# Scan phase: the feed-forward weight quantised in its turned layout, its scales brought back as rows through memory

## The chip, the cores and the metric

The kernel runs on one core of one Trainium2 chip. The metric is the device time of one execution in microseconds; the median of the runs shown is used. The profile is of one execution, recorded by the hardware profiler.

## The reference, cut to what matters

Two layers work on x, 2 x 4096 tokens of 512 channels. The first adds to x a gated state-space branch and a quantised linear map; the second is a linear attention with a gated feed-forward part. The change touches only how the weight of the quantised map is prepared:

```
xn = layernorm(x)
x  = x + _L0_attn_ref(xn, ...) + _L0_ffn_ref(xn, weight, bias)

# in _L0_ffn_ref: weight is [512 out, 512 in]
blocks = weight.reshape(512, 16, 32)                  # blocks of 32 along the input channel
scales = maximum(max(abs(blocks), axis=-1) / 7.5, 1e-30)
wd     = nearest_on_fp6_grid(blocks / scales) * scales
out    = xd @ wd.T + bias                             # xd: the input, quantised in the same way
```

The product contracts over the input channel, so TensorE wants the weight with the input channel on the partitions ("turned"), while a block of 32 lies along the input channel.

## The kernel before, in words

Four phases run one after the other on each engine: project (the first two weight products), scan (the state-space recurrence), mix (the sums of layer one and the first half of layer two) and the second layer. The change is in the scan phase, phase_scan (L648 to L915).

The scan loops over 64 octets o of 8 channels each. TensorE makes three f32 products per octet, each 128x128 by 128x512: `own` of the next octet (L885, into bank SB), the Toeplitz product (L903) and the product with the states (L906, both into bank YB). In program order they are own(o+1), L903 of o, L906 of o. VectorE scans the bank of own(o+1) into c_state (L757, two instructions); L906 of octet o+1 waits for them. ScalarE takes the finished bank out (`take`, L827) and issues the store of it to scr_y (L831) on its own DMA queue. GpSimd writes the three masked tables of an octet (L739), three octets ahead at most; own(o) waits for the tables of o. SyncE loads z (L701) six octets ahead.

Everything else of the scan phase is hung onto octets by constants, at the end of an octet's step on the engine in question. VectorE's step of octet o is: the scan of o+1 first, then what hangs on o. So a wait in what hangs on o holds up the scan of o+2. ScalarE's step of octet o is take(o), then DMA issues and copies that hang on o, then the store of o.

The feed-forward weight in this scheme:
- ScalarE loads it in its natural layout, output channel on the partitions, in four DMAs of 256 KB (L844) at o = 1 to 4, into c_wf_nat, [128, 2048].
- VectorE quantises it in nine steps at o = 10 to 18 (L771 to L794): the maximum over blocks of 32 (L776), scale (L778), reciprocal (L780), the product with the inverse scale (L782), exponent bits (L784), rounding constant (L787), addition (L789), subtraction (L791), product with the scale (L793). L784 and L787 have one tensor as input, L782, L789, L791 and L793 two.
- TensorE turns it at o = 24 to 27 (`turn_weight`, L888): four transposes of 128x128 an octet into one of the banks 0 to 3.
- ScalarE copies each bank as the high part of the split weight one octet later (L860), VectorE subtracts it for the low part another octet later (L808).
- The weights w2 and wk are split in the same way from SBUF at o = 32 to 39 (L836 and L762). Their pieces, and those of wv, are loaded by ScalarE at every second octet from o = 6 to 28 (L854).
- GpSimd clears two accumulators and a column at its octet 20 (L743).

Of the kernel before, what the change touches and what calls it, by code (L numbers as in the profile page):

```python
# [3 lines left out]
P = 128  # L4
# [643 lines left out]
def phase_scan(nc, sh, ins, scr, keep, banks, areas, late, mix):  # L648
# [5 lines left out]
    def sem(name):  # L654
        return nc.alloc_semaphore(name)
# [9 lines left out]
    q_scale = first_weight.tile("c_q_scale", [P, KT * D // QBLOCK])  # L665
    q_inv = first_weight.tile("c_q_inv", [P, KT * D // QBLOCK])
# [3 lines left out]
    w2_raw, wk_raw = late["w2_raw"], late["wk_raw"]  # L670

    z_in = [sem(f"c_z_in{i}") for i in range(Z)]
    y_stored = [sem(f"c_y_stored{i}") for i in range(Y)]
# [5 lines left out]
    wf_in = sem("c_wf_in")  # L679
    w_hi, w_lo = keep["w_hi"], keep["w_lo"]  # L680
    HI = 2 * KT
    q_step, f_turned, f_hi = sem("c_q_step"), sem("c_f_turned"), sem("c_f_hi")

    FB, YB, SB = banks[0:4], banks[4:6], banks[6:8]
    into_t, toep_t, out_pow, mask8 = keep["into_t"], keep["toep_t"], keep["out_pow"], keep["mask8"]
    ident = keep["ident"]
    z_of = scr["z"].rearrange("(o c) r n -> o (c r) n", c=OCTET)
    y_of = scr["y"].rearrange("(o c) m n -> o (c m) n", c=OCTET)
    TURN_AT, WEIGHTS_AT, QUANTISE_AT = 24, 32, 10
    QUANTISED_AT, WEIGHT_PIECES_AT, BIASES_AT = 1, 6, 30  # L690
    MIX_IN_AT, MIX_PREPARE_AT, MIX_BANKS_AT, MIX_HEAD_AT = 38, 40, 42, 61
    MIX_TURN_AT = {56: 0, 60: 1}
# [57 lines left out]
    def vector(dve):  # L750
        def scan(o):
            dve.wait_ge(own_full, o + 1)
            if o >= 2:
                dve.wait_ge(y_full, o - 1)
            rate = keep["decay"][:, o:o + 1].broadcast_to([P, NCB - 1])
            for b in range(B):
                nc.vector.tensor_tensor_scan(state[o % 2][:, b, 1:], rate, SB[o % 2][:, b * NCB:(b + 1) * NCB - 1],  # L757
                                             0.0, ALU.mult, ALU.add).then_inc(state_done, 1)

        def weight_low(i, kt, tile, raw):  # L760
            dve.wait_ge(w_hi, HI + KT * i + kt + 1)
# [3 lines left out]
        blocks = wf_nat[:, :].rearrange("p (b e) -> p b e", e=QBLOCK)  # L765
        NB = KT * D // QBLOCK

        def wide(tile):
            return tile[:, :].unsqueeze(2).broadcast_to([P, NB, QBLOCK])

        def quantise_step(k):  # L771
            dve.wait_ge(wf_in, 16 * KT)
            if k:
                dve.wait_ge(q_step, k)
            if k == 0:
                ins_ = nc.vector.tensor_reduce(q_max[:, :], blocks, AX.X, ALU.max, apply_absolute_value=True)  # L776
            elif k == 1:
                ins_ = nc.vector.tensor_scalar(q_scale[:, :], q_max[:, :], 1.0 / FP6_MAX, SCALE_EPS, ALU.mult, ALU.max)  # L778
            elif k == 2:
                ins_ = nc.vector.reciprocal(q_inv[:, :], q_scale[:, :])  # L780
            elif k == 3:
                ins_ = nc.vector.tensor_tensor(blocks, blocks, wide(q_inv), ALU.mult)  # L782
            elif k == 4:
                ins_ = nc.vector.tensor_scalar(q_work[:, :].bitcast(U32), wf_nat[:, :].bitcast(U32), EXPONENT_BITS,  # L784
                                               None, ALU.bitwise_and)
            elif k == 5:
                ins_ = nc.vector.tensor_scalar(q_work[:, :], q_work[:, :], 1.0, ROUND_MAGIC, ALU.max, ALU.mult)  # L787
            elif k == 6:
                ins_ = nc.vector.tensor_tensor(wf_nat[:, :], wf_nat[:, :], q_work[:, :], ALU.add)  # L789
            elif k == 7:  # L790
                ins_ = nc.vector.tensor_tensor(wf_nat[:, :], wf_nat[:, :], q_work[:, :], ALU.subtract)  # L791
            else:
                ins_ = nc.vector.tensor_tensor(blocks, blocks, wide(q_scale), ALU.mult)  # L793
            ins_.then_inc(q_step, 1)  # L794

        for i in range(2):
            nc.vector.memset(state[i][:, :, 0:1], 0.0).then_inc(zeroed, 1)
        dve.wait_ge(zeroed, 2)
        scan(0)
        for o in range(NO):  # L800
            if o + 1 < NO:
                scan(o + 1)
            if QUANTISE_AT <= o < QUANTISE_AT + 9:
                quantise_step(o - QUANTISE_AT)
            if TURN_AT <= o - 2 < TURN_AT + KT:
                kt = o - 2 - TURN_AT
                dve.wait_ge(f_hi, kt + 1)
                nc.vector.tensor_tensor(wf[:, 1, kt, :], FB[kt][:, :], wf[:, 0, kt, :].bitcast(F32), ALU.subtract)\  # L808
# [12 lines left out]

    def scalar(act):
# [17 lines left out]
        for o in range(NO):  # L840
            take(o)
            if QUANTISED_AT <= o < QUANTISED_AT + KT:
                t = o - QUANTISED_AT
                act.dma_start(wf_nat[:, t * D:(t + 1) * D], ins["L0_ffn_weight"][t * P:(t + 1) * P, :])\  # L844
                   .then_inc(wf_in, 16)
            if o == WEIGHT_PIECES_AT:
                for h in range(2):
                    act.wait_ge(*project["z"][h])
                    act.wait_ge(*project["v"][h])
                act.wait_ge(*project["powers"])  # L850
            if WEIGHT_PIECES_AT <= o < WEIGHT_PIECES_AT + 2 * 3 * KT and (o - WEIGHT_PIECES_AT) % 2 == 0:
                i, kt = divmod((o - WEIGHT_PIECES_AT) // 2, KT)
                tile, name, done = pieces[i]
                act.dma_start(tile[:, kt, :], ins[name][:, kt, :]).then_inc(done, 16)  # L854
            if o in (BIASES_AT, BIASES_AT + 2, BIASES_AT + 4):
                mix["load_bias"]((o - BIASES_AT) // 2)
            if TURN_AT <= o - 1 < TURN_AT + KT:
                kt = o - 1 - TURN_AT
                act.wait_ge(f_turned, kt + 1)
                nc.scalar.activation(wf[:, 0, kt, :], FB[kt][:, :], ACT.Copy).then_inc(f_hi, 1)  # L860
            if WEIGHTS_AT <= o < WEIGHTS_AT + 2 * KT:
                i, kt = divmod(o - WEIGHTS_AT, KT)
                weight_high(i, kt, *((w2, w2_raw), (wk, wk_raw))[i])
# [1274 lines left out]
def two_layer_kernel(nc, ins, out):  # L2138
# [3 lines left out]
    def dram(name, shape, dt=F32):  # L2142
# [118 lines left out]
```

## Time and profile before

| | us |
|---|---|
| median of 3 runs (2083.98 to 2085.03) | 2084.08 |
| the profiled execution, its own time | 2084.98 |
| its span, first to last instruction | 2083.2 |
| TensorE busy in it | 2065.6 |
| VectorE busy in it | 1521.2 |
| ScalarE busy in it | 1095.3 |
| GpSimd busy in it | 839.5 |

Span and busy times are of the profiled execution; 1.8 us of its time lie around the span, and it is 0.9 us longer than the median. A matmul in f32 is recorded as two instructions, so its rows say x2, and a row's duration is to the end of the last one, beyond the start of the next.

### The profile page before, as it was taken

The numbers are of one execution on the slowest core, as the hardware profiler recorded it, in microseconds if no ns is written. First come the engines' busy times: TensorE is split into PE (matmuls) and PEld (weight loads), VectorE is DVE, ScalarE is ACT, GpSimd is POOL, SyncE is SP. The second block draws the span as 40 slices with busy tenths as digits, with TensorE's granted clock in tenths as the row PEclk, the third lists the DMA queues.
The fourth block names the chain that finished last, engine by engine and source line by source line (L and its number), as shares of the span: only waits on it lengthen the run. The fifth ranks groups of instructions, "written<-read, shape, count | busy, mean of one in ns | idle before, by whom it ended". The sixth has DMA issues, their size and how long they took to land.

```text
span 2083.2 us, 27336 instructions
## 1 busy us (share of the span) xinstructions
PE 2065.6 (99%) x9263; PEld 1647.1 (79%) x9263; DVE 1521.2 (73%) x2943; ACT 1095.3 (53%) x1842; POOL 839.5 (40%) x842
## 2 busy tenths in 40 slices
PE   9999999999999999999999999999999999999998
PEld 7787888444688888888888888788888888888887
DVE  5898785666687777777777875677777676667776
ACT  4555556323455555555555555754455555555453
POOL 1001110355545444454445453144444444444444
PEclk9999999999999999999999999999999999999999
DMA  5997883886533333333333333422222222222211
GB/s 186 235 222 221 202 219 116 280 255 211 178 115 118 102 118 105 116 118 102 122 107 117 103 128 104 152 71 72 71 71 71 92 91 81 92 71 72 71 41 41
DMA packets 193637, 263.46 MB, mean 126 GB/s; under 512 B 34265, under 2 KB 124633, under 8 KB 190938
## 3 DMA queue, kind: packets, MB, share of 16 engines
q1 hardware_dynamic: 180376, 238.18, 37.7%
q10 hardware_dynamic: 13122, 23.53, 3.0%
q8 instruction: 74, 1.21, 0.2%
q14 instruction: 65, 0.53, 0.1%
HBM read 160.88 MB, written 100.79 MB: 126 GB/s over the span
## 4 chain that ended last, share of the span: by engine, by line
PE 89%; DVE 5%; ACT 2%; issue 2%; POOL 1%; DMA 1%; SPq 0%; POOLq 0%; ACTq 0%
PE bank L102 23%; PE bank L104 23%; PE bank L103 22%; PE bank L1496 7%; PE bank L2052 3%; PE bank L885 3%; PE bank L906 3%; PE bank L903 3%; PE bank L1452 2%; PE bank L629 1%; DVE e_w_lo L1879 0%; DVE d_x L1348 0%; DVE d_xq L1319 0%; DVE d_stats L1350 0%; PE bank L1510 0%
## 5 line engine op out<-in xcount | busy, mean ns | idle before, releaser
L102 PE MATMUL bank<-e_ring,e_w_hi 128*128 128x512 f32 x512 | 200.8, 392 | 0.0
L103 PE MATMUL bank<-e_ring,e_w_hi 128*128 128x512 f32 x512 | 199.3, 389 | 0.0
L104 PE MATMUL bank<-e_ring,e_w_lo 128*128 128x512 f32 x512 | 199.3, 389 | 0.0
L1496 PE MATMUL bank<-d_kh,d_nat 128*128 128x512 f32 x768 | 191.1, 398 | 0.0
L1772 POOL TENSOR_TENSOR e_x<-e_x,e_beta 128x512 f32<-128x512 f32 x64 | 91.3, 1446 | 220.7 <-ACT e_y L1815 220.7
L1117 POOL TENSOR_TENSOR rstd<-d_var_eps,neg_half 128x1 f32<-128x1 f32 x64 | 35.6, 556 | 340.5 <-DVE d_var_eps L1359 340.5
L1826 ACT ACTIVATE e_kr<-bank 128x512 f32<-128x512 f32 x64 | 38.0, 593 | 247.6 <-PE bank L104 247.6
L1496 PEld LDWEIGHTS bank<-d_kh,d_nat 128*128 128x128 f32 x768 | 139.7, 188 | 26.9
L1897 DVE TENSOR_TENSOR e_ring<-e_mixed,e_ring 128x512 fp32r<-128x512 f32 x128 | 93.5, 731 | 88.1 <-ACT e_ring L1790 88.0
L1754 POOL TENSOR_TENSOR e_x<-e_x,e_ff 128x512 f32<-128x512 f32 x64 | 83.3, 1302 | 175.6 <-DVE e_ff L1963 175.6
L1364 DVE TENSOR_TENSOR d_nat<-d_xn,d_nat 128x512 fp32r<-128x512 f32 x64 | 85.9, 1344 | 77.7 <-ACT d_nat L1224 77.7
L1888 DVE SCALAR_TENSOR_TENSOR e_mixed<-e_xt,cols,e_prev 128x512 f32<-128x512 f32 x128 | 104.0, 813 | 41.3 <-ACT e_prev L1801 40.7
L1206 ACT ACTIVATE d_xt<-bank 128x512 f32<-128x512 f32 x64 | 38.2, 597 | 166.9 <-PE bank L1452 166.9
L757 DVE TENSOR_TENSOR_SCAN c_state<-decay,bank 128x255 f32<-128x255 f32 x128 | 80.5, 670 | 52.8 <-PE bank L885 52.6
L308 POOL TENSOR_TENSOR b_rstd<-b_var_eps,neg_half 128x4 f32<-128x4 f32 x16 | 16.2, 1010 | 255.0 <-DVE b_var_eps L364 255.0
L102 PEld LDWEIGHTS bank<-e_ring,e_w_hi 128*128 128x128 f32 x512 | 96.1, 188 | 20.4 <-issue 0.9
L1790 ACT ACTIVATE e_ring<-e_mixed 128x512 fp32r<-128x512 f32 x128 | 80.7, 632 | 59.8 <-DVE e_mixed L1888 57.5
L1758 POOL TENSOR_TENSOR e_y<-e_y,e_att 128x512 f32<-128x512 f32 x64 | 107.0, 1671 | 12.8 <-DVE e_att L1982 12.8
L104 PEld LDWEIGHTS bank<-e_ring,e_w_lo 128*128 128x128 f32 x512 | 96.1, 188 | 20.0
L103 PEld LDWEIGHTS bank<-e_ring,e_w_hi 128*128 128x128 f32 x512 | 96.1, 188 | 19.3
L102 PE MATMUL bank<-e_w_hi,e_keys 128*128 128x512 f32 x256 | 103.7, 405 | 0.1
L102 PE MATMUL bank<-b_xt,b_v 128*128 128x512 f32 x256 | 100.8, 394 | 2.7 <-ACT b_vt L557 2.7
(222 smaller groups left out, 6298.0 us busy)
## 6 DMA issues: line engine op xcount, KB each, us to landing
scr_v<-b_vt SPq DMA_DIRECT2D x64, 256.0 KB, 3.5
scr_z<-b_zt SPq DMA_DIRECT2D x64, 256.0 KB, 5.6
c_z<-scr_z SPq DMA_DIRECT2D x64, 256.0 KB, 4.3
scr_y<-c_y ACTq DMA_DIRECT2D x64, 256.0 KB, 3.9
d_x<-in_L_attn_x SPq DMA_DIRECT2D x64, 256.0 KB, 3.8
d_v<-scr_v SPq DMA_DIRECT2D x32, 512.0 KB, 5.1
scr_x<-d_x SPq DMA_DIRECT2D x64, 256.0 KB, 2.3
scr_xnt<-d_xt SPq DMA_DIRECT2D x32, 512.0 KB, 4.1
```

The lines of the kernel that those rows point to most:

```text
L102: eng.matmul(out, lhs[hi], rhs[hi], start=first, stop=False, skip_group_check=onto)
L103: eng.matmul(out, lhs[hi], rhs[lo], start=False, stop=False, skip_group_check=onto)
L104: return eng.matmul(out, lhs[lo], rhs[hi], start=False, stop=last, skip_group_check=onto)
L757: nc.vector.tensor_tensor_scan(state[o % 2][:, b, 1:], rate, SB[o % 2][:, b * NCB:(b + 1) * NCB - 1], 0.0, ALU.mult, ALU.add).then_inc(sta ...
L1364: nc.vector.tensor_tensor(nat[q][:, 1, :], xn[N % 2][:, :], nat[q][:, 0, :].bitcast(F32), ALU.subtract).then_inc(nat_lo, 1)
L1496: mm = pe.matmul(BG[c][:, :], s[:, i, cols], r[:, j, :], start=M % NTB == 0 and i == j, stop=M % NTB == NTB - 1 and i == 1, skip_group_che ...
L1754: nc.gpsimd.tensor_tensor(x2[h][:, t, :], x2[h][:, t, :], ff[t % 2][:, :], ALU.add).then_inc(base_done, 1)
L1758: nc.gpsimd.tensor_tensor(y[t][:, :], y[t][:, :], att[t % 2][:, :], ALU.add).then_inc(sum_done, 1)
L1772: nc.gpsimd.tensor_tensor(x2[h][:, t, :], x2[h][:, t, :], beta[:, :], ALU.add).then_inc(shifted, 1)
L1790: nc.scalar.activation(ring[slot][:, 0, kt, :], src, ACT.Copy).then_inc(hi_done, 1)
L1888: nc.vector.scalar_tensor_tensor(mixed[kt % 2][:, :], current(g % 2, kt), mu[:, kt:kt + 1], prev[kt % 2][:, :], ALU.mult, ALU.add).then_in ...
L1897: nc.vector.tensor_tensor(ring[slot][:, 1, kt, :], src, ring[slot][:, 0, kt, :].bitcast(F32), ALU.subtract).then_inc(lo_done, 1)
```

## The change

The host lays the weight out a second time, turned (input channel on the partitions), as the input ffn_turned. The natural copy is still loaded, but serves for the maxima alone.

- VectorE finds the maxima at o = 14 (the same instruction), the scales in four small instructions at o = 15, the inverse scales at o = 16, and at o = 17 turns both in 32x32 blocks with four `transpose` instructions into c_q_turned.
- ScalarE loads the turned weight in four DMAs of 256 KB at o = 7, 9, 11, 13. At o = 18 it stores the turned scales in four DMAs of 16 KB to a new scratch tensor, scr_f_scales [32, 512]. At o = 20 it waits for these stores and issues two loads of 1 MB each: rows of the inverse scales into c_q_work and rows of the scales into c_wf_nat, each of 4 rows of 8 KB, repeated for 32 partitions.
- VectorE quantises the turned weight in six steps at o = 22 to 27, of the same kinds as the last six before; the first waits for both row loads.
- ScalarE and VectorE split it at o = 29 to 33, from SBUF. The sixteen transposes on TensorE are gone, and banks 0 to 3 are not used in the scan by them.

```diff
-    TURN_AT, WEIGHTS_AT, QUANTISE_AT = 24, 32, 10
+    ROUNDED_AT, WEIGHTS_AT, SCALES_AT, SCALES_OUT_AT, ROWS_IN_AT, QUANTISE_AT = 28, 32, 14, 18, 20, 22
+    SCALE_STEPS, QUANTISE_STEPS = 3 + KT, 6
+        def scale_step(k):
+            if k:
+                dve.wait_ge(q_step, min(k, 3))
+            scales = q_cols[:, :, KT * KT:2 * KT * KT]
+            if k == 0:
+                dve.wait_ge(wf_in, 32 * KT)
+                ins_ = nc.vector.tensor_reduce(q_max[:, :], wf_nat[:, :].rearrange("p (b e) -> p b e", e=QBLOCK), AX.X,
+                                               ALU.max, apply_absolute_value=True)
...
+            elif k == 2:
+                ins_ = nc.vector.reciprocal(q_cols[:, :, 0:KT * KT], scales)
+            else:
+                ins_ = nc.vector.transpose(q_turned[:, k - 3, :], q_cols[:, k - 3, :])
+            ins_.then_inc(q_step, 1)
         def quantise_step(k):
+            dve.wait_ge(q_step, SCALE_STEPS + k)
+            wf_turned = wf_raw[:, :, :].rearrange("p k d -> p (k d)")
             if k == 0:
+                dve.wait_ge(wf_in, 16 * (2 * KT + KT + 2))
+                ins_ = nc.vector.tensor_tensor(wf_turned, wf_turned, q_work[:, :], ALU.mult)
             elif k == 1:
+                ins_ = nc.vector.tensor_scalar(q_work[:, :].bitcast(U32), wf_turned.bitcast(U32), EXPONENT_BITS,
+                                               None, ALU.bitwise_and)
...
             else:
+                ins_ = nc.vector.tensor_tensor(wf_turned, wf_turned, wf_nat[:, :], ALU.mult)
...
+            if o == SCALES_OUT_AT:
+                act.wait_ge(q_step, SCALE_STEPS)
+                for s in range(P // QBLOCK):
+                    act.dma_start(scr["f_scales"].rearrange("c (t s i) -> s c t i", t=KT, s=P // QBLOCK)[s],
+                                  q_turned[s * QBLOCK:(s + 1) * QBLOCK, :, :]).then_inc(wf_in, 16)
+            if o == ROWS_IN_AT:
+                act.wait_ge(wf_in, 16 * (2 * KT + KT))
+                for w, tile in enumerate((q_work, wf_nat)):
+                    rows = bass.AP(scr["f_scales"].tensor, w * KT * KT * D,
+                                   [[KT * D, P // QBLOCK], [0, QBLOCK], [1, KT * D]])
+                    act.dma_start(tile[:, :], rows).then_inc(wf_in, 16)
...
+            if WEIGHT_PIECES_AT <= o < WEIGHT_PIECES_AT + 2 * KT and (o - WEIGHT_PIECES_AT) % 2:
+                kt = (o - WEIGHT_PIECES_AT) // 2
+                act.dma_start(wf_raw[:, kt, :], ins["ffn_turned"][:, kt, :]).then_inc(wf_in, 16)
...
-                act.wait_ge(f_turned, kt + 1)
-                nc.scalar.activation(wf[:, 0, kt, :], FB[kt][:, :], ACT.Copy).then_inc(f_hi, 1)
+                act.wait_ge(q_step, SCALE_STEPS + QUANTISE_STEPS)
+                nc.scalar.activation(wf[:, 0, kt, :], wf_raw[:, kt, :], ACT.Copy).then_inc(f_hi, 1)
...
-        def turn_weight(kt):
-            if kt == 0:
-                pe.wait_ge(q_step, 9)
-            for ot in range(KT):
-                mm = pe.transpose(FB[kt][:, ot * P:(ot + 1) * P], wf_nat[:, ot * D + kt * P:ot * D + (kt + 1) * P],
-                                  ident[:, :])
-            mm.then_inc(f_turned, 1)
...
-            if TURN_AT <= o < TURN_AT + KT:
-                turn_weight(o - TURN_AT)
...
+        "f_scales": dram("scr_f_scales", [QBLOCK, D]),
...
+    laid["ffn_turned"] = raw["L0_ffn_weight"].T.reshape(KT, P, 512).transpose(1, 0, 2)
```

## Rows read from the trace of the kernel before

**Rows 1.** The page: busy time by engine, and the chain that ended last.

```profile
PE 2065.6 (99%) x9263; PEld 1647.1 (79%) x9263; DVE 1521.2 (73%) x2943; ACT 1095.3 (53%) x1842; POOL 839.5 (40%) x842
...
PE 89%; DVE 5%; ACT 2%; issue 2%; POOL 1%; DMA 1%; SPq 0%; POOLq 0%; ACTq 0%
```

**Rows 2.** Timeline, TensorE: start, duration, line, count [idle before, releaser].

```profile
376.14 1.02 PE L906 MATMUL bank<-c_state,c_outof 128*128 128x512 f32 x2
...
407.04 1.02 PE L906 MATMUL bank<-c_state,c_outof 128*128 128x512 f32 x2
...
412.19 1.02 PE L906 MATMUL bank<-c_state,c_outof 128*128 128x512 f32 x2
413.48 1.10 PE L885 MATMUL bank<-c_z,c_into 128*128 128x512 f32 x2 [0.27 <-issue]
...
430.34 1.02 PE L906 MATMUL bank<-c_state,c_outof 128*128 128x512 f32 x2
...
441.50 0.60 PE L892 MATMUL bank<-consts,c_wf_nat 128*128 128x128 f32 x4
441.93 1.02 PE L885 MATMUL bank<-c_z,c_into 128*128 128x512 f32 x2
```

**Rows 3.** Timeline, VectorE, while the weight is quantised.

```profile
407.56 0.53 DVE L780 RECIPROCAL c_q_inv<-c_q_scale 128x64 f32<-128x64 f32 x1
408.95 1.26 DVE L757 TENSOR_TENSOR_SCAN c_state<-decay,bank 128x255 f32<-128x255 f32 x2 [0.87 <-PE bank L885]
410.13 2.26 DVE L782 TENSOR_TENSOR c_wf_nat<-c_wf_nat,c_q_inv 128x2048 f32<-128x2048 f32 x1
412.31 1.25 DVE L757 TENSOR_TENSOR_SCAN c_state<-decay,bank 128x255 f32<-128x255 f32 x2
413.49 1.33 DVE L784 TENSOR_SCALAR c_q_work<-c_wf_nat 128x2048 uint32<-128x2048 uint32 x1
...
415.91 1.20 DVE L787 TENSOR_SCALAR c_q_work<-c_q_work 128x2048 f32<-128x2048 f32 x1
...
418.36 2.27 DVE L789 TENSOR_TENSOR c_wf_nat<-c_wf_nat,c_q_work 128x2048 f32<-128x2048 f32 x1
...
421.72 2.40 DVE L791 TENSOR_TENSOR c_wf_nat<-c_wf_nat,c_q_work 128x2048 f32<-128x2048 f32 x1
...
425.21 2.26 DVE L793 TENSOR_TENSOR c_wf_nat<-c_wf_nat,c_q_scale 128x2048 f32<-128x2048 f32 x1
```

**Rows 4.** Timeline, GpSimd, two of the table products.

```profile
400.42 0.40 POOL L739 TENSOR_TENSOR c_into<-into_t,consts 128x128 f32<-128x128 f32 x1 [1.46 <-PE bank L906]
...
410.72 1.94 POOL L739 TENSOR_TENSOR c_into<-into_t,consts 128x128 f32<-128x128 f32 x1 [1.46 <-PE bank L906]
```

**Rows 5.** The lines that make the low parts of the split weights, VectorE.

```profile
L808 DVE TENSOR_TENSOR d_wf<-bank,d_wf x4: 662/664/667, 447.2 to 455.8; 128x512 fp32r<-128x512 f32 x4
...
L762 DVE TENSOR_TENSOR d_w<-d_w_raw,d_w x4: 691/691/693, 465.2 to 472.9; 128x512 fp32r<-128x512 f32 x4
```

**Rows 6.** Timeline, ScalarE: a take and the DMA issue that hangs on it.

```profile
408.10 0.60 ACT L827 ACTIVATE c_y<-bank 128x512 f32<-128x512 f32 x1 [1.98 <-PE bank L906]
408.10 0.35 ACTq L854 DMA_DIRECT2D d_w_raw<-in_L_attn_w_w  x1
```

**Rows 7.** DMA issues: count, KB each, median us to landing.

```profile
c_z<-scr_z SPq DMA_DIRECT2D x64, 256.0 KB, 4.3
...
e_w_raw<-in_L_attn_Wq SPq DMA_DIRECT2D x1, 1024.0 KB, 5.0
...
scr_rows<-mean SPq DMA_DIRECT2D x14, 2.0 KB, 11.6
```

**Rows 8.** Stretches: busy us (instructions), TensorE's granted clock, DMA share, GB/s.

```profile
62.00:66.00 4.00, 4.00 (x12) 3.17 (x11) 3.93 (x6) 1.74 (x3) 0.00 (x0) 0.57 0.97 210
66.00:70.00 4.00, 4.00 (x20) 3.26 (x19) 3.93 (x4) 2.08 (x4) 0.00 (x0) 1.00 1.03 388
```

**Rows 9.** Timeline, TensorE, the idle time ahead of the first of these.

```profile
61.42 0.50 PE L102 MATMUL bank<-b_xt,b_v 128*128 128x512 f32 x1 [2.72 <-ACT b_vt L557]
```

More of the change, by code:

```diff
@@ L664, in phase_scan @@
     q_max = first_weight.tile("c_q_max", [P, KT * D // QBLOCK])
-    q_scale = first_weight.tile("c_q_scale", [P, KT * D // QBLOCK])
-    q_inv = first_weight.tile("c_q_inv", [P, KT * D // QBLOCK])
+    q_cols = first_weight.tile("c_q_cols", [P, KT, QBLOCK])
+    q_turned = first_weight.tile("c_q_turned", [P, KT, QBLOCK])
     wf_nat = turned_x.tile("c_wf_nat", [P, KT * D])
@@ L669, in phase_scan @@
     w2, wf, wk, wv = late["w2"], late["wf"], late["wk"], late["wv"]
-    w2_raw, wk_raw = late["w2_raw"], late["wk_raw"]
+    w2_raw, wf_raw, wk_raw = late["w2_raw"], late["wf_raw"], late["wk_raw"]
     z_in = [sem(f"c_z_in{i}") for i in range(Z)]
@@ L681, in phase_scan @@
     HI = 2 * KT
-    q_step, f_turned, f_hi = sem("c_q_step"), sem("c_f_turned"), sem("c_f_hi")
-    FB, YB, SB = banks[0:4], banks[4:6], banks[6:8]
+    q_step, f_hi = sem("c_q_step"), sem("c_f_hi")
+    YB, SB = banks[4:6], banks[6:8]
     into_t, toep_t, out_pow, mask8 = keep["into_t"], keep["toep_t"], keep["out_pow"], keep["mask8"]
-    ident = keep["ident"]
     z_of = scr["z"].rearrange("(o c) r n -> o (c r) n", c=OCTET)
     y_of = scr["y"].rearrange("(o c) m n -> o (c m) n", c=OCTET)
-    TURN_AT, WEIGHTS_AT, QUANTISE_AT = 24, 32, 10
+    ROUNDED_AT, WEIGHTS_AT, SCALES_AT, SCALES_OUT_AT, ROWS_IN_AT, QUANTISE_AT = 28, 32, 14, 18, 20, 22
+    SCALE_STEPS, QUANTISE_STEPS = 3 + KT, 6
     QUANTISED_AT, WEIGHT_PIECES_AT, BIASES_AT = 1, 6, 30
@@ L763, in weight_low @@
                                     ALU.subtract).then_inc(w_lo, 1)
[L765 to L769, printed above, removed]
+        def scale_step(k):
[6 more added lines that the diff above has]
+                                               ALU.max, apply_absolute_value=True)
+            elif k == 1:
+                for t in range(KT):
+                    ins_ = nc.vector.tensor_scalar(scales[:, t, :].rearrange("p (s k) -> p k s", k=KT),
+                                                   q_max[:, t * KT * KT:(t + 1) * KT * KT]
+                                                   .rearrange("p (k s) -> p k s", k=KT),
+                                                   1.0 / FP6_MAX, SCALE_EPS, ALU.mult, ALU.max)
+            elif k == 2:
[3 more added lines that the diff above has]
+            ins_.then_inc(q_step, 1)
@@ L771, in quantise_step @@
         def quantise_step(k):
-            dve.wait_ge(wf_in, 16 * KT)
-            if k:
-                dve.wait_ge(q_step, k)
+            dve.wait_ge(q_step, SCALE_STEPS + k)
+            wf_turned = wf_raw[:, :, :].rearrange("p k d -> p (k d)")
             if k == 0:
-                ins_ = nc.vector.tensor_reduce(q_max[:, :], blocks, AX.X, ALU.max, apply_absolute_value=True)
+                dve.wait_ge(wf_in, 16 * (2 * KT + KT + 2))
+                ins_ = nc.vector.tensor_tensor(wf_turned, wf_turned, q_work[:, :], ALU.mult)
@@ L777, in quantise_step @@
             elif k == 1:
-                ins_ = nc.vector.tensor_scalar(q_scale[:, :], q_max[:, :], 1.0 / FP6_MAX, SCALE_EPS, ALU.mult, ALU.max)
+                ins_ = nc.vector.tensor_scalar(q_work[:, :].bitcast(U32), wf_turned.bitcast(U32), EXPONENT_BITS,
+                                               None, ALU.bitwise_and)
             elif k == 2:
-                ins_ = nc.vector.reciprocal(q_inv[:, :], q_scale[:, :])
+                ins_ = nc.vector.tensor_scalar(q_work[:, :], q_work[:, :], 1.0, ROUND_MAGIC, ALU.max, ALU.mult)
@@ L781, in quantise_step @@
             elif k == 3:
-                ins_ = nc.vector.tensor_tensor(blocks, blocks, wide(q_inv), ALU.mult)
+                ins_ = nc.vector.tensor_tensor(wf_turned, wf_turned, q_work[:, :], ALU.add)
             elif k == 4:
[L784 to L791, printed above, removed]
+                ins_ = nc.vector.tensor_tensor(wf_turned, wf_turned, q_work[:, :], ALU.subtract)
@@ L792, in quantise_step @@
             else:
-                ins_ = nc.vector.tensor_tensor(blocks, blocks, wide(q_scale), ALU.mult)
+                ins_ = nc.vector.tensor_tensor(wf_turned, wf_turned, wf_nat[:, :], ALU.mult)
             ins_.then_inc(q_step, 1)
@@ L802, in vector @@
                 scan(o + 1)
-            if QUANTISE_AT <= o < QUANTISE_AT + 9:
+            if SCALES_AT <= o < SCALES_AT + 3:
+                scale_step(o - SCALES_AT)
+            if o == SCALES_AT + 3:
+                for k in range(3, SCALE_STEPS):
+                    scale_step(k)
+            if QUANTISE_AT <= o < QUANTISE_AT + QUANTISE_STEPS:
                 quantise_step(o - QUANTISE_AT)
-            if TURN_AT <= o - 2 < TURN_AT + KT:
-                kt = o - 2 - TURN_AT
+            if ROUNDED_AT <= o - 2 < ROUNDED_AT + KT:
+                kt = o - 2 - ROUNDED_AT
                 dve.wait_ge(f_hi, kt + 1)
-                nc.vector.tensor_tensor(wf[:, 1, kt, :], FB[kt][:, :], wf[:, 0, kt, :].bitcast(F32), ALU.subtract)\
+                nc.vector.tensor_tensor(wf[:, 1, kt, :], wf_raw[:, kt, :], wf[:, 0, kt, :].bitcast(F32), ALU.subtract)\
                   .then_inc(w_lo, 1)
@@ L854, in scalar @@
                 act.dma_start(tile[:, kt, :], ins[name][:, kt, :]).then_inc(done, 16)
+            if WEIGHT_PIECES_AT <= o < WEIGHT_PIECES_AT + 2 * KT and (o - WEIGHT_PIECES_AT) % 2:
+                kt = (o - WEIGHT_PIECES_AT) // 2
+                act.dma_start(wf_raw[:, kt, :], ins["ffn_turned"][:, kt, :]).then_inc(wf_in, 16)
             if o in (BIASES_AT, BIASES_AT + 2, BIASES_AT + 4):
                 mix["load_bias"]((o - BIASES_AT) // 2)
-            if TURN_AT <= o - 1 < TURN_AT + KT:
-                kt = o - 1 - TURN_AT
-                act.wait_ge(f_turned, kt + 1)
-                nc.scalar.activation(wf[:, 0, kt, :], FB[kt][:, :], ACT.Copy).then_inc(f_hi, 1)
+            if ROUNDED_AT <= o - 1 < ROUNDED_AT + KT:
+                kt = o - 1 - ROUNDED_AT
+                act.wait_ge(q_step, SCALE_STEPS + QUANTISE_STEPS)
+                nc.scalar.activation(wf[:, 0, kt, :], wf_raw[:, kt, :], ACT.Copy).then_inc(f_hi, 1)
             if WEIGHTS_AT <= o < WEIGHTS_AT + 2 * KT:
```

## The prediction

> **What bounds the kernel now.** I read the busy times and the chain first: TensorE is busy for 99% of the span and carries 89% of the chain [rows 1]. So work taken off TensorE counts in full, and time in which TensorE is kept waiting counts in full too. Next the timeline of TensorE in the scan. Its L906 of octet 0 starts at 376.14 and that of octet 12 at 407.04 [rows 2]: 30.90 / 12 = 2.575 us an octet with no gap, three products of 0.858 us. TensorE sets the pace, and L906 of octet o starts at 376.14 + 2.575 o as long as nothing is late. Call this the undisturbed clock.
>
> Two things disturb it before. From L906 of octet 14 (412.19) to that of octet 20 (430.34) 18.15 us pass [rows 2], where six octets take 15.45: **2.70 us are lost** while the long quantising steps run. The rows beside it say why. A table product of GpSimd takes 0.40 us, but the one that starts at 410.72 takes 1.94 and ends when VectorE's L782 ends [rows 3, 4]; the next own starts 1.29 us after L906 instead of 0.86 [rows 2]. L885 is said to wait for "issue", but the tables are what came last. Secondly the transposes: four of them stand 0.43 us in TensorE's row, 441.50 to 441.93 [rows 2], and there are four such groups, **1.72 us**. Together 4.4 us that the change could win at most.
>
> **Part by part.**
>
> The transposes go: -1.72 us, at once, since nothing but TensorE's own work sets those four octets.
>
> The maxima, scales and inverse scales move by four octets. VectorE has 2.575 - 1.18 = 1.39 us an octet beside the scan, whose pitch is 408.95 to 410.13 [rows 3]. A reciprocal of 64 columns takes 0.53 us [rows 3]. The three small scalings more and the four block transposes of 32 columns each are not in the trace; from below nothing, from above 0.53 us each, which would be 2.1 us for the transposes at o = 17. VectorE may run about 1.9 us late before L906 is kept waiting (below), so even that end costs nothing in front of an octet with no step behind it. I take 0.
>
> ScalarE gets ten more DMA issues at 0.35 us [rows 6] and waits twice. Its octet holds 0.60 + 0.35 to 0.70 us of 2.575 [rows 6], so issues are covered. The wait at o = 18 is for VectorE's transposes, which come right after scan(18); it is over before take(18). The wait at o = 20 is for four stores of 128-byte pieces, issued 5 us earlier. Nearest rows: 4.3 us for 256 KB, and 11.6 us for 2 KB in 4-byte pieces [rows 7]. I take the first, as pieces of 128 bytes are 32 times larger than the slow ones; the other end is rival C. Behind that wait stand take(21) and the row loads.
>
> The high and low parts are read from SBUF: VectorE's 0.664 becomes 0.691 us [rows 5], under the same 1.39 us. 0.
>
> The row loads and the first quantising step are the new wait. ScalarE issues the loads with take(20). A take starts 1.06 us after L906 (408.10 against 407.04 [rows 2, 6]), so the issue is at 376.14 + 51.50 + 1.06 = 428.7. VectorE asks for them after scan(23), which starts 1.91 us after L906 of octet 21 (408.95 against 407.04 for octet 12 [rows 2, 3]): 376.14 + 54.08 + 1.91 + 1.18 = 433.3. So **they have 4.6 us to land** before VectorE stops. Then VectorE needs 2.19 us for the product (410.13 to 412.31 [rows 3]) and 1.18 for scan(24); L906 of octet 24 is due at 376.14 + 61.80 = 437.9. TensorE is therefore kept waiting if the loads land after 437.9 - 3.4 = 434.5, or 5.8 us after issue.
>
> They are 2.1 MB. One load of 1 MB lands 5.0 us after its issue [rows 7]. The DMA engines at full share move 388 / 1.03 = 376 GB/s, 23.5 GB/s each of 16 [rows 8]; 1.05 MB is 2.8 us of that, leaving 2.2 us that don't depend on size. Two ends then:
> - spread over 16 engines: 2.2 + 2.10 MB / 376 GB/s = 7.8 us, and with three z loads in between (0.7 us each by the same rate) 9.9;
> - spread over 4 engines: 2.2 + 2.10 / 94 = 24.5 us, with four z loads 27.3.
>
> Every large load of the trace has 128 entries in the outermost dimension at both ends, and reaches the rate of 16 engines. The row loads' source has **4 entries outermost**, each repeated 32 times. If a transfer is dealt out by its outermost dimension, only four shares exist, and engines 5 to 16 get none. No row here shows a transfer with four; I take this end, 25 us, because the only thing in which these loads differ from the row of 5.0 us is just that dimension.
>
> The Trainium skill states this rule in "DMA: Bandwidth & Descriptors", section "Rules for kernel authors": an outermost dimension of size c below 16 confines the whole DMA to at most c engines. By it the loads land some 25 us after issue; by the row of 5.0 us alone, 8 to 10.
>
> Working it out for 25 us: landing 428.7 + 25.0 = 453.7; product and scan 2.19 + 1.18, and 0.1 to L906: 457.2, against 437.9 due: **19.3 us lost**. From there VectorE is the bound for five octets: steps of 1.33, 1.20, 2.27, 2.40, 2.26 us, each 0.08 less in pitch, plus 5 scans of 1.18 = 15.0 us [rows 3], against 5 x 2.575 = 12.9: **2.1 us**. GpSimd's lengthened tables fall into the same octets; TensorE already waits there for VectorE, so I add nothing for them, where before they made the 2.70.
>
> **The clock.** TensorE idles some 19 us in this wait. After an idle 2.72 us [rows 9] the granted clock was 0.57 in the next stretch of 4 us and 1.00 after it [rows 8], that is 0.43 x 4 = 1.7 us of work lost, at the lower level of 1.2 GHz. The two octets right behind the wait have short steps on VectorE, so little of it is covered: **1.6 us**.
>
> Sum: 19.3 + 2.1 + 1.6 - 2.70 - 1.72 = **+18.6 us**. The profiled execution took 2084.98, so 2103.6 for one like it; the median of before is 0.9 lower, which gives 2102.7.
>
> **Rivals.**
>
> A. The loads run on 16 engines. Place: the same wait of VectorE at o = 22. They land after 7.8 to 9.9 us, and L906 of octet 24 is late by 2.0 to 4.1, then 2.1 as above, and at the upper end 1.6 for the clock: 4.1 to 7.8 lost, less 4.4: -0.3 to +3.4, or 2083.8 to 2087.5. That is not slower by more than the 0.2% (4.2 us) that a measurement of this kernel can tell from no change. It decides if the loads land within about 11 us of issue. For it: all MB-sized loads here take 5 us or so [rows 7]. Against it: the four outer entries.
>
> B. The loads even land within 5.8 us, and only the transposes show: the six steps then lose about what they lost before, 2.6 us, and the gain is 1.7: 2082.4. Against it: 2.1 MB at 376 GB/s alone is 5.6 us.
>
> C. The stores of the scales land like the 4-byte ones, 11.6 us after issue [rows 7]. The last is issued at about 425.4, so the wait of ScalarE ends at 437.0, 8.3 us after 428.7; takes and row loads shift by that: 2111 with four engines, 2094 to 2096 with sixteen.
>
> D. The change doesn't keep TensorE free: only if a transpose stayed. The diff leaves none; no chance given.
>
> **Chances.** Forecast 0.79, A 0.12, B 0.02, C 0.07. The forecast's own range comes from 22 us to landing and no loss by the clock (-3.0 - 1.6: 2098) to 27.3 us and a low clock for twice as long (+2.3 + 1.6: 2106.6). I widen it by 3 us below, for a rate per engine that is higher when only four are at work, and up to C: 2095 to 2111. A and B lie outside. Slower by over 0.2%: the forecast, C and a tail of A, 0.87. Within 0.2%: 0.11. Faster: 0.02, since the whole of what could be won, 4.4 us, is just over the bound.
>
> **What would show it.** In the changed profile: no L892 rows; one idle time of TensorE of 15 to 21 us ahead of L906 of octet 24, released by c_state, and VectorE's product waiting for the DMA into c_wf_nat or c_q_work; these loads with 22 to 27 us to landing; a DMA share of about a quarter in that stretch; a granted clock near 0.5 for some us behind it. The loss at octets 14 to 20 should be gone. I am wrong on the main step if the row loads land within 11 us, and on the others if TensorE also stops at octet 20 or 21 (the stores), or if the six steps lose well over 2 us behind the wait.

## The result, and the profile after

The changed kernel takes 2112.55 us (median of 4 runs, 2108.96 to 2114.83) against 2084.03 for the one before in the same comparison: ratio 1.0139, 95% interval 1.0127 to 1.0151, so 1.4% slower. The profiled execution took 2110.73 (span 2108.9), which is 25.75 more than the profiled one of before.

The page of the kernel after, busy times and chain [rows 1]:

```profile
PE 2066.7 (98%) x9247; PEld 1647.0 (78%) x9247; DVE 1520.9 (72%) x2950; ACT 1095.4 (52%) x1842; POOL 837.0 (40%) x842
...
PE 88%; DVE 5%; DMA 2%; ACT 2%; issue 2%; POOL 1%; SPq 0%; POOLq 0%; ACTq 0%; DVEq 0%
```

TensorE's work has not grown; 2% of the chain is now a transfer. Where it stands shows in TensorE's timeline. The numbering has moved: L927 is the product with the states (before: L906), L914 own, L924 the Toeplitz product [rows 2].

```profile
373.90 1.02 PE L927 MATMUL bank<-c_state,c_outof 128*128 128x512 f32 x2
...
412.53 1.02 PE L927 MATMUL bank<-c_state,c_outof 128*128 128x512 f32 x2
...
417.56 1.12 PE L927 MATMUL bank<-c_state,c_outof 128*128 128x512 f32 x2 [2.29 <-DVE c_state L757]
...
440.16 1.12 PE L924 MATMUL bank<-c_z,c_toep 128*128 128x512 f32 x2 [0.90 <-ACT c_y L842]
465.09 2.08 PE L927 MATMUL bank<-c_state,c_outof 128*128 128x512 f32 x2 [23.81 <-DVE c_state L757]
```

I call **slip** the start of that product in octet o, less its start in octet 0 and less 2.575 o: zero on the undisturbed clock. After: 0 up to octet 15 (412.53), 2.46 at 16, 4.26 at 18 to 23 (the second part, 1.80, comes under a low clock; see the stretches below), 29.39 at 24 (465.09), 33.14 at 29, 33.81 at 63. Before, it ends at 5.12. So the scan lost 28.69 us; the phase before it happened to end 2.24 us earlier (octet 0 at 373.90 against 376.14), the phases behind it took 0.70 less, and 28.69 - 2.24 - 0.70 = 25.75.

VectorE, after, with the two stops and the six steps [rows 3]:

```profile
414.05 2.29 DVE L772 TENSOR_REDUCE c_q_max<-c_wf_nat 128x64 f32<-128x2048 f32 x1 [3.49 <-DMA d_wf_raw<-in_ffn_turned]
...
417.42 0.39 DVE L776 TENSOR_SCALAR c_q_cols<-c_q_max 128x16 f32<-128x16 f32 x4
...
421.42 0.47 DVE L783 STREAM_TRANSPOSE c_q_turned<-c_q_cols 128x32 f32<-128x32 f32 x4
...
461.58 2.29 DVE L792 TENSOR_TENSOR d_wf_raw<-d_wf_raw,c_q_work 128x2048 f32<-128x2048 f32 x1 [26.17 <-DMA c_wf_nat<-scr_f_scales]
463.79 1.25 DVE L757 TENSOR_TENSOR_SCAN c_state<-decay,bank 128x255 f32<-128x255 f32 x2
464.96 1.20 DVE L794 TENSOR_SCALAR c_q_work<-d_wf_raw 128x2048 uint32<-128x2048 uint32 x1
```

The maxima wait 3.49 us for a load of the *turned* weight, which they don't read. The product waits 26.17 us for the rows. ScalarE, after, from the stores of the scales on [rows 6]:

```profile
425.57 2.64 ACTq L864 DMA_DIRECT2D scr_f_scales<-c_q_turned  x4
...
430.72 0.60 ACT L842 ACTIVATE c_y<-bank 128x512 f32<-128x512 f32 x1 [0.68 <-PE bank L927]
430.72 0.60 ACTq L871 DMA_DIRECT2D c_q_work<-scr_f_scales  x1
431.36 0.56 ACTq L871 DMA_DIRECT2D c_wf_nat<-scr_f_scales  x1
...
434.19 5.21 ACTq L846 DMA_DIRECT2D scr_y<-c_y  x1
...
439.52 4.21 ACTq L880 DMA_DIRECT2D d_wv<-in_L_attn_Wv  x1
443.78 3.87 ACTq L846 DMA_DIRECT2D scr_y<-c_y  x1
```

The row loads are issued at 430.72 and the product begins at 461.58, 30.9 us later. In the trace the packets of 8 KB are the rows: 256 of them on ScalarE's queue, the first starts at 433.09, the last ends at 460.96. Stretches, after: the last columns are TensorE's granted clock, the DMA share and GB/s [rows 8].

```profile
418.70:422.15 3.45, 3.45 (x5) 1.36 (x5) 2.35 (x8) 0.60 (x1) 1.12 (x3) 0.51 0.66 188
...
430.00:435.00 5.00, 5.00 (x13) 2.28 (x12) 2.37 (x5) 1.23 (x3) 2.25 (x6) 1.00 0.94 267
...
450.00:455.00 5.00, 0.00 (x0) 0.00 (x0) 0.00 (x0) 0.00 (x0) 0.00 (x0) 0.50 0.37 141
455.00:460.00 5.00, 0.00 (x0) 0.00 (x0) 0.00 (x0) 0.00 (x0) 0.00 (x0) 0.50 0.24 103
460.00:465.00 5.00, 0.00 (x0) 0.00 (x0) 3.42 (x4) 0.00 (x0) 0.00 (x0) 0.50 0.21 80
```

Ahead of the landing the DMA share is 0.24, about 4 engines of 16, at 103 GB/s: the four shares of the prediction, seen.

### The profile page after: what moved, and what is told of

It is laid out like the page before. It is cut to its first block, busy times and chain, and to the rows that moved or that the text cites. A ratio compares the mean times of both kernels' runs of the same rounds, so it can differ in the third digit from the quotient of the medians.

```text
span 2108.9 us, 27314 instructions
## 1 busy us (share of the span) xinstructions
PE 2066.7 (98%) x9247; PEld 1647.0 (78%) x9247; DVE 1520.9 (72%) x2950; ACT 1095.4 (52%) x1842; POOL 837.0 (40%) x842
## 4 chain that ended last, share of the span: by engine, by line
PE 88%; DVE 5%; DMA 2%; ACT 2%; issue 2%; POOL 1%; SPq 0%; POOLq 0%; ACTq 0%; DVEq 0%
PE bank L102 23%; PE bank L104 22%; PE bank L103 22%; PE bank L1515 7%; PE bank L2071 3%; PE bank L927 2%; PE bank L914 2%; PE bank L924 2%; PE bank L1471 2%; DMA c_wf_nat<-scr_f_scales 1%; PE bank L629 1%; DVE e_w_lo L1898 0%; DVE d_x L1367 0%; DVE d_xq L1338 0%; DVE d_stats L1369 0%
## 5 line engine op out<-in xcount | busy, mean ns | idle before, releaser
L842 ACT ACTIVATE c_y<-bank 128x512 f32<-128x512 f32 x64 | 38.2, 596 | 145.8 <-PE bank L927 129.6
L103 PEld LDWEIGHTS bank<-e_ring,e_w_hi 128*128 128x128 f32 x512 | 96.2, 188 | 19.3
```

The lines of the kernel that those rows point to most:

```text
L103: eng.matmul(out, lhs[hi], rhs[lo], start=False, stop=False, skip_group_check=onto)
```

## The experiments

In each, the slip is read as above, from the one profiled execution. Those marked "one time" have a single time and no interval; the others are medians of 4 to 11 executions. A ratio is to the kernel before, timed in the same comparison, with its 95% interval.

**rows_16**: each load of 4 x 32 rows becomes four loads of 32 partitions, whose outermost dimension has 32 entries.

```diff
-                    rows = bass.AP(..., w * KT * KT * D, [[KT * D, P // QBLOCK], [0, QBLOCK], [1, KT * D]])
-                    act.dma_start(tile[:, :], rows).then_inc(wf_in, 16)
+                    for s in range(P // QBLOCK):
+                        rows = bass.AP(..., (w * KT + s) * KT * D, [[0, QBLOCK], [1, KT * D]])
+                        act.dma_start(tile[s * QBLOCK:(s + 1) * QBLOCK, :], rows).then_inc(wf_in, 16)
```

> Each row load of 1 MB is cut into four of 32 partitions, so that the outermost dimension is 32 and not 4; bytes, rows and repeats are the same. Theory (a load is dealt out by its outermost dimension, four entries use four DMA engines): all eight land 8 to 10 us after the first issue instead of 31, TensorE's wait ahead of L906's counterpart of octet 24 falls from 24 to 2 to 4 us, and the kernel takes 2088 to 2093 us (the stop at octet 16 stays). Rival (reading one row 32 times, or sharing with the z loads and y stores, makes the loads slow): they land 25 to 31 us after issue as before and the time stays at 2105 to 2115.

Measured: 2096.57, ratio 1.006 (1.0043 to 1.0076), 16.0 us below the change; slip 4.18 at octet 17, 15.54 at 24, 19.94 at 63. The time lies above my range of 2088 to 2093 and below the rival's 2105. The outermost dimension is the main cause, but a stop of 11.4 us stays where I had worked out 2.0 to 4.1 for sixteen engines.

**rows_2** (one time): the opposite, two loads of 64 partitions for each tile, outermost dimension 2 (`[[KT * D, 2], [0, QBLOCK], [1, KT * D]]`).

> The opposite dose: each row load is cut into two of 64 partitions, whose source has 2 entries outermost. Theory: all run on the same two engines, the data need twice as long, the last load lands 50 to 60 us after issue and the kernel takes 2130 to 2145 us. Rival (bytes or repeats set it): landing and time as in the changed kernel, 2109 to 2115.

Measured: 2130.23; slip 53.40 at octet 63. The stretch of rows_2 behind the start of the stop:

```profile
440.00:445.00 5.00, 0.00 (x0) 0.00 (x0) 0.00 (x0) 0.00 (x0) 0.00 (x0) 0.64 0.13 42
```

A share of 0.13 is 2 engines of 16. Its slip comes in two parts, as TensorE's timeline of rows_2 shows:

```profile
458.03 2.07 PE L925 MATMUL bank<-c_z,c_toep 128*128 128x512 f32 x2 [22.04 <-ACT c_y L842]
...
484.35 2.08 PE L928 MATMUL bank<-c_state,c_outof 128*128 128x512 f32 x2 [20.72 <-DVE c_state L757]
```

The first wait is not for the rows but for ScalarE's take of y, whose queue is held up; the next runs show by what.

**own_sem**: the turned loads count on a semaphore of their own, so that neither the maxima nor the row loads wait for them.

```diff
-                dve.wait_ge(wf_in, 32 * KT)
+                dve.wait_ge(wf_in, 16 * KT)
...
-                act.dma_start(wf_raw[:, kt, :], ins["ffn_turned"][:, kt, :]).then_inc(wf_in, 16)
+                act.dma_start(wf_raw[:, kt, :], ins["ffn_turned"][:, kt, :]).then_inc(turned_in, 16)
```

> The turned weight's loads count on a semaphore of their own, so that the maxima at octet 14 wait for the natural weight alone; the row loads stay as they are. Theory: the stop of 2.3 us ahead of octet 16 and the low clock behind it go, 4.3 us in all: 2106 to 2110 us. Rival (VectorE is late there for the reduction itself, or the clock falls for another reason): octet 16 and 17 still lose 2 us or more and the time stays at 2109 to 2115.

Measured: 2112.01, ratio 1.0138: nothing gained, outside my range of 2106 to 2110. The rival is not it either, as octets 16 and 17 lose nothing now. The stop at octet 16 is gone, but the slip at octet 24 is 29.34, against 29.39 without the edit. VectorE and ScalarE of own_sem:

```profile
462.96 2.29 DVE L793 TENSOR_TENSOR d_wf_raw<-d_wf_raw,c_q_work 128x2048 f32<-128x2048 f32 x1 [30.37 <-DMA c_wf_nat<-scr_f_scales]
```

```profile
427.90 0.60 ACTq L872 DMA_DIRECT2D c_q_work<-scr_f_scales  x1
...
432.30 5.16 ACTq L847 DMA_DIRECT2D scr_y<-c_y  x1
```

From issue to product it is 35.1 us now, 4.2 more: what the loads gained in start they lost on the way. Why is open. It is not that more octets run beside them: in both kernels they are issued with take(20) and TensorE stops ahead of octet 24. Between issue and product the packets of all other transfers moved 3.10 MB in the changed kernel and 3.17 MB here, nearly the same.

**rows_16_own_sem**: both edits.

> Both together. Theory: what is left is a wait of 2 to 4 us at octet 24, some 2 us behind it for the six steps, perhaps 1.6 us of low clock, against 4.4 us that the kernel before loses: 2084 to 2088 us. Rival (the two stops overlap, or a third wait takes their place): over 2090.

Measured: 2092.75, ratio 1.0042 (1.0027 to 1.0057); slip 8.84 at octet 24, 13.24 at 63. That is over the 2084 to 2088 of my theory: the stop at octet 24 still costs 8.5 us. With the short landing the semaphore is worth 3.8 us by the medians of two sets of four executions (these reach from 2089.6 to 2095.74), and 6.7 by the slips of the profiled ones; alone it was worth nothing.

**distinct_rows** (one time): as the last, but the loads read 32 different rows of the turned weight instead of one row 32 times. The scales are left out of its product.

> As rows_16_own_sem, but the eight loads of 256 KB read 128 different rows of 8 KB (the turned weight itself) in place of four rows 32 times over. What is left out: the scales, so the quantised weight is another. Theory (the repeats slow the reads: all engines ask for the same 8 KB): packets of 8 KB take 310 to 350 ns instead of 560, the last load lands 8 to 10 us after the first issue instead of 14, TensorE's stop at octet 24 is 2 to 5 us instead of 8.5. Rival (z loads, y stores and the number of issues set it): the stop stays at 7 to 9 us.

Measured: 2094.19; slip 11.48 at octet 24. No faster, and the packets of 8 KB take 550 ns in the mean against 546 in rows_16_own_sem, so my theory that the repeats of one row cost the time fell.

**full_rows** (one time): as own_sem, but two loads of all 128 different rows of the turned weight, outermost dimension 128. The scales are left out again.

> As own_sem, but each of the two loads of 1 MB reads 128 different rows of the turned weight, so that it has 128 entries outermost at both ends and fills all 128 partitions at once. What is left out: the scales. Theory (behind the 14 us of the eight loads of 32 partitions stands their destination: all 16 engines write the same 32 partitions at a time): packets of 8 KB take 310 to 350 ns instead of 550, both loads land 8 to 10 us after the first issue, TensorE's stop at octet 24 is 2 to 4 us. Rival (z loads and y stores beside them set it, whatever the destination): 12 to 14 us to landing and a stop of 8 us.

Measured: 2087.75; slip 5.80 at octet 24, 10.21 at 63. The packets of 8 KB take 344 ns in the mean, inside the 310 to 350 foreseen, though the stop is longer than the 2 to 4 us. The same stretch of distinct_rows, of rows_16_own_sem and of full_rows, last columns share and GB/s:

```profile
430.00:435.00 5.00, 5.00 (x13) 2.03 (x12) 1.26 (x2) 1.20 (x2) 2.25 (x6) 1.00 1.00 246
```

```profile
430.00:435.00 5.00, 4.94 (x12) 1.82 (x10) 0.21 (x1) 1.79 (x3) 2.25 (x6) 1.00 1.00 220
```

```profile
430.00:435.00 5.00, 5.00 (x13) 2.22 (x12) 0.97 (x2) 1.19 (x2) 2.09 (x7) 1.00 0.99 373
```

All engines are busy in all three, but 220 to 246 GB/s are moved with loads into 32 partitions and 373 with loads into 128. The row packets alone, over the time from the first to the last of them, come to 179 GB/s (rows_16_own_sem) and 151 (distinct_rows) against 233 (full_rows). full_rows also has two issues in place of eight; that was not tried by itself, but with a share of 0.99 to 1.00 in all three no engine stood without work.

The Trainium skill has this in "SBUF — State Buffer", section "Door 1: The DMA port swizzle": partitions 0 to 31 reach 8 of the 16 ports through which DMA reaches SBUF, about 218 GB/s at most, and all 128 reach 16. The trace agrees: the row packets stay below 218 into 32 partitions, at 179 and 151, and exceed it into 128, at 233; the 220 and 246 hold other traffic too. My rival A reckoned with the full rate for such loads.

**rows_16_early**: as rows_16_own_sem, with the maxima at octet 8 and the rows issued at 14 instead of 20; the first product stays at 22.

```diff
-    ..., SCALES_AT, SCALES_OUT_AT, ROWS_IN_AT, QUANTISE_AT = 28, 32, 14, 18, 20, 22
+    ..., SCALES_AT, SCALES_OUT_AT, ROWS_IN_AT, QUANTISE_AT = 28, 32, 8, 12, 14, 22
```

> As rows_16_own_sem, with the scales computed at octets 8 to 11, stored at 12 and the row loads issued at 14, eight octets (20 us) ahead of their use instead of two. Theory (what costs is the wait alone): no stop at octet 24; the six long steps lose 2.6 us as before, the transposes' 1.7 us are won: 2081.5 to 2084. Rival (the slow reads on ScalarE's DMA queue hold the y stores behind them, and takes four octets on wait): a new stop of 1 to 4 us at octets 16 to 19, time 2084 to 2088.

Measured: 2090.78, ratio 1.0034 (1.0021 to 1.0047). The place is the rival's, the size is beyond both ranges: no stop at octet 24, but slips of 7.00 at 20 and 9.09 at 24, 11.37 at the end. ScalarE of rows_16_early shows why:

```profile
431.67 0.60 ACT L843 ACTIVATE c_y<-bank 128x512 f32<-128x512 f32 x1 [10.12 <-DMA scr_y<-c_y]
```

The take waits for an older store of y to free its buffer, and that store stands behind 2 MB of row loads. TensorE waits 4.1 us for such takes and 1.4 us for z.

**rows_4_early** (one time): own_sem with the unchanged two loads issued at 14 and first used at 26.

> The two loads of 1 MB with four entries outermost, unchanged, but issued at octet 14 and used at 26, 30 us ahead. Theory (on four engines of ScalarE's DMA queue they hold up what is issued behind them, y stores first, and ScalarE itself cannot issue): an early issue does not hide them; TensorE stops for a bank that ScalarE has not taken, 10 to 20 us around octets 17 to 20, and the time stays over 2095. Rival (only VectorE's wait costs): no stop, 2081 to 2085.

Measured: 2108.14; slip 25.49 at octet 20, 28.81 at 63. TensorE of rows_4_early:

```profile
450.56 2.07 PE L925 MATMUL bank<-c_z,c_toep 128*128 128x512 f32 x2 [13.36 <-ACT c_y L843]
```

Twelve octets of lead buy almost nothing: 2108.14, one time, against 2112.01 for own_sem. The three waits of TensorE for such takes add up to 21.8 us. The loads do their harm by what they hold up, not only by what waits for them.

**rows_paced**: as rows_16_early, but the eight loads of 256 KB are issued one an octet, at octets 14 to 21; quantising starts at 24.

```diff
-            if o == ROWS_IN_AT:
+            if ROWS_IN_AT <= o < ROWS_IN_AT + 2 * P // QBLOCK:
+                w, s = divmod(o - ROWS_IN_AT, P // QBLOCK)
...
+                act.dma_start((q_work, wf_nat)[w][s * QBLOCK:(s + 1) * QBLOCK, :], rows).then_inc(wf_in, 16)
```

> The eight loads of 256 KB (own semaphore, scales at octets 8 to 11) are issued one an octet at octets 14 to 21, so that each y store stands behind one of them only; the six steps come at octets 24 to 29. Theory (what the early issue cost was the y stores held behind 2 MB on ScalarE's queue): no stop of TensorE at octets 16 to 24; the six steps lose 2.7 us, the transposes' 1.7 us are won: 2081.5 to 2084. Rival (the added 2 MB beside z, y and the weight pieces fill the DMA engines however they are spread): takes wait for y stores or own for z, 1 us or more, 2084 to 2088.

Measured: 2084.02, ratio 0.9997 (0.9988 to 1.0005), no difference from before. No stop up to octet 24; slip 4.09 at 63, of which 3.33 by octet 31 with the six steps. Takes did wait for y stores, 4.5 us in all, but without delay for TensorE. And 1.37 of the 3.33 come at octet 26, where VectorE of rows_paced waits once more for the last row load:

```profile
441.31 2.29 DVE L793 TENSOR_TENSOR d_wf_raw<-d_wf_raw,c_q_work 128x2048 f32<-128x2048 f32 x1 [2.40 <-DMA c_wf_nat<-scr_f_scales]
```

**before_spread**: the kernel before, with its nine quantising steps in every second octet (`(o - QUANTISE_AT) % 2 == 0`) and the transposes at 27.

> The kernel before with its nine quantising steps on every second octet (10 to 26) and the transposes at 27 to 30. Theory (the 2.7 us are lost because long steps follow each other and hold up GpSimd's tables and the scans): 0 to 1.5 us of it stay, the time falls to 2081.5 to 2083. Rival (each long step costs by itself, 0.45 us as one table product is held 1.5 us): 2 us or more stay, no change in time.

Measured: 2083.19, ratio 0.9994 (0.9984 to 1.0003), slip 4.02 against 5.12. By octet 31 the slip is 3.34, where before had 4.46. With 1.76 of each for the transposes, the steps lose 1.58 instead of 2.70: 0.5 each at octets 18, 24 and 26. The fourth piece falls to octet 28, where the first transposes fill the time in which TensorE would wait. So the loss lies just above my 0 to 1.5, and the time can't tell it from no change. GpSimd of before_spread, where an undisturbed table takes 0.40 [rows 4], and VectorE's step beside the first of them:

```profile
425.10 0.87 POOL L739 TENSOR_TENSOR c_into<-into_t,consts 128x128 f32<-128x128 f32 x1 [0.96 <-PE bank L906]
...
435.40 1.94 POOL L739 TENSOR_TENSOR c_into<-into_t,consts 128x128 f32<-128x128 f32 x1 [1.45 <-PE bank L906]
441.06 1.94 POOL L739 TENSOR_TENSOR c_into<-into_t,consts 128x128 f32<-128x128 f32 x1 [1.91 <-PE bank L906]
```

```profile
424.52 1.20 DVE L784 TENSOR_SCALAR c_q_work<-c_wf_nat 128x2048 uint32<-128x2048 uint32 x1
```

A single two-input step of 2.3 us costs 0.5 us through the table that it holds, with no long step next to it. The one-input steps of 1.20 us hold a table as well, for 0.87, and cost nothing. So the length of such a step decides first: four pieces of 0.5 are 2.0, and that the steps follow each other adds the other 0.7 of before. The kind of step matters too: beside the maxima, which take 2.26 us, the tables of before take 0.40.

**paced_half**: rows_paced with each step as two of 1024 columns, at octets 24 to 35.

> As rows_paced, with each of the six steps done in two halves of 1024 columns, one half an octet at octets 24 to 35. Theory (a table product of GpSimd held by a step of 1.2 us still ends in time, one held by 2.3 us costs TensorE 0.5 us): the six steps lose 0 to 0.6 us instead of 2.7: 2079.5 to 2081.5. Rival (a held table product costs as often as there are steps): 2 us or more stay.

Measured: 2081.79, ratio 0.9986 (0.9975 to 0.9997). VectorE of paced_half ahead of its first half step:

```profile
440.29 1.43 DVE L797 TENSOR_TENSOR d_wf_raw<-d_wf_raw,c_q_work 128x1024 f32<-128x1024 f32 x1 [3.85 <-issue]
```

Slip 1.96 at octet 26, and only 2.06 from there to 34: the halves themselves cost nearly nothing there. The time lies 0.3 us above my range, with that stop in it.

**paced_two**: as paced_half, but the first half step waits for the four loads of inverse scales alone, the last pair for the other four.

```diff
-                dve.wait_ge(wf_in, 16 * (KT + KT + 8))
+                dve.wait_ge(inverse_in, 16 * KT)
...
+                if h == 0:
+                    dve.wait_ge(wf_in, 16 * 3 * KT)
                 ins_ = nc.vector.tensor_tensor(wt, wt, nat, ALU.mult)
```

> As paced_half, but the first half step waits only for the four loads of inverse scales (issued at octets 14 to 17), and the four loads of scales (octets 18 to 21) are waited for at the last step pair. In paced_half VectorE stood 3.85 us ahead of its first half step and TensorE was kept waiting 1.8 us ahead of L906 of octet 26. Theory (that stop is the wait for the last row load): it goes whole, the slip stays under 0.7 us up to octet 34, and the time is 1.5 to 2 us below paced_half's 2081.8, so 2079.8 to 2080.5. Rival (the stop is due to something else beside it, such as c_z or the y stores being held behind the loads): the slip of 1.5 to 2 us at octet 26 stays, and the time is 2081.5 to 2082.

Measured: 2080.43 (2078.61 to 2081.98), ratio 0.9984 (0.9975 to 0.9993). The slip is 0.00 up to octet 34 and 1.62 at 43 to 56. VectorE of paced_two, the first half step, and GpSimd beside it:

```profile
437.37 1.20 DVE L797 TENSOR_TENSOR d_wf_raw<-d_wf_raw,c_q_work 128x1024 f32<-128x1024 f32 x1
438.77 1.26 DVE L757 TENSOR_TENSOR_SCAN c_state<-decay,bank 128x255 f32<-128x255 f32 x2 [0.20 <-PE bank L921]
```

```profile
437.95 0.88 POOL L739 TENSOR_TENSOR c_into<-into_t,consts 128x128 f32<-128x128 f32 x1 [1.45 <-PE bank L934]
```

The stop was the wait for the last row load; the rival fell. A held table lasts 0.88 here instead of 1.94, and costs nothing. Of the 1.62, 0.64 come at octets 41 to 43 in every kernel, before too (4.46 to 5.10), and are not due to the change. The rest begins with 0.42 at octet 35, when the last half steps run beside the split of w2; why was not tried by itself. This is the fastest version measured, 0.16% below before. Its intervals overlap with those of paced_half, so between these two only the slip of one execution each decides.

## Why the prediction was wrong

The forecast was 2102.7, range 2095 to 2111; 2112.55 lies 1.6 us above the range. The sign and the main mechanism were right: one stop of VectorE at its first product, at octet 24, released by the row loads, on a quarter of the engines. By steps, against the sum (+18.6 foreseen, +28.69 in the scan):

- **Transposes and quantising loss, -4.42 foreseen.** No transposes stand in the trace after, and no loss is at octets 14 to 20 but the one below. Of the 5.12 of before, 4.46 had come by octet 28. Right.
- **Scales, block transposes, issues, 0 foreseen.** Four scalings take 0.39 us together, four block transposes 0.47. Four store issues take 2.64, so 0.66 each and not 0.35, but the slip is constant at 4.26 from octet 18 to 23. Right.
- **Rival C.** The wait for the stores is over by 430.72, with no slip at octets 21 to 23. It did not happen.
- **The maxima "move by four octets", no wait foreseen.** The first failed step. The maxima count to 32 x KT on a semaphore which the turned loads also raise, up to octet 13, so VectorE waits 3.49 us for a load it doesn't read. TensorE idles 2.29, and then runs at 0.51 of its clock for 3.45 us, at the lower level, 1.2 GHz: 4.26 us of slip. The diff shows the count; I costed the instruction and not what its wait had come to mean.
- **"Landing 25 us after issue, 19.3 us lost".** The second failed step: the size of the main term. It took 30.9 us, and the octet lost 25.13. The rate per engine was not to blame: at the end 103 GB/s on a share of 0.24 is 27 GB/s for each of about four engines, above my 23.5. While the rows run alone (452 to 458) a packet of 8 KB takes 309 ns; 64 for each of four engines would be done in 19.8 us (an estimate from these). They took 27.9, from 433.09 to 460.96, with 2.19 MB of other packets between them. So about 8 us went to sharing, where I had at most 2.8, for four z loads, and nothing for y stores and weight pieces. Which of the other packets went through these four engines, and how much each kind adds, was not separated. own_sem shows how little an earlier issue buys: issued 4.3 us earlier as counted from octet 0, the loads took 4.2 us longer, and why is open.
- **Six steps 2.1 and clock 1.6, 3.7 together.** Measured 29.39 to 33.14, 3.75. Right in sum; the 2.49 of octet 25 hold the low clock.

4.26 + 5.83 (25.13 - 19.3) = 10.1 is the whole difference between the two sums. But the two are not independent, as own_sem shows: without the first stop the second grows by the same amount, and the time stays at 2112.01. So what failed in the total is the time to landing.

I also wrote that the outermost dimension was the only thing in which these loads differ from the row of 5.0 us. They read each row 32 times as well; distinct_rows shows, on sixteen engines, that this costs nothing.

**Rival A was too cheap.** With sixteen engines and 128 partitions (full_rows) the stop at octet 24 is 5.8 us, where I said 2.0 to 4.1, and the kernel takes 2087.75, just above my 2083.8 to 2087.5, although it has no stop at octet 16. With 32 partitions at a time, the way in which repeated rows were spread here, it is 8.8 us.

The working also left out what is late next on ScalarE's queue. The y stores stand behind the rows, and takes wait for their buffers. In rows_2 and rows_4_early that is about 22 us; after, TensorE waited for it only 0.90 us before VectorE's wait stopped it.

## What to carry to other kernels

Read the outermost dimension of every new large load and the number of partitions it writes: both set its rate here. Large loads on a queue that also carries a steady stream of stores whose buffers are needed again (256 KB each here) delay that stream whether or not anybody waits for the load, so hand them out one a loop step rather than early and at once, and let each user wait only for the loads that it reads (paced_two). When a semaphore gets a second user, work out again what each old count on it now waits for.

## What the runs showed of the hardware

- The share of DMA engines at work follows the outermost count: 0.24 at four entries (after) and 0.13 at two (rows_2). This is the rule of "DMA: Bandwidth & Descriptors" in the Trainium skill, section "Rules for kernel authors": with an outermost dimension of c below 16 a DMA runs on at most c engines.
- With sixteen busy engines, 220 to 246 GB/s were moved while the loads wrote 32 partitions at a time, 373 while they wrote 128. A packet of 8 KB took 546 to 550 ns against 344.
- The issue of a DMA on ScalarE's queue, 0.33 to 0.66 us otherwise, took 5.21, 4.21 and 3.87 us while the four-engine loads were under way, and the next take began only behind the issue. In rows_16_early, whose loads run on sixteen engines, no issue took over 0.80.
- A VectorE quantising step from SBUF held the GpSimd table product beside it until 0.25 to 0.27 us after its own end: 1.94 us beside a two-input step with 2048 columns (2.26 us), 0.88 beside one with 1024 (1.20 us), 0.87 beside a one-input step with 2048 (1.20 us), 0.40 without. The first cost 0.5 us of TensorE's time, the others none at octets 15 to 34. Beside the maxima of 2.26 us the tables took 0.40.
- TensorE idled 2.29 us ahead of octet 16; 1.2 us after it had started again, its granted clock fell to the lower level of 1.2 GHz (0.51) for 3.45 us. The idle time had cost 2.46 us of slip, and the low clock took 1.80 more.
